# First stage of a four-stage transformer kernel: block inversion moved from VectorE to GpSimd, an instruction order per engine, and smaller stages on TensorE

## The chip, the cores and the metric

The kernel runs on one core of a Trainium2 chip. Its time is the device time of one execution in microseconds (us); shown are the median and the extremes of several runs. Engines: TensorE (PE; its weight loads are PEld in the profile), VectorE (DVE), ScalarE (ACT), GpSimd (POOL) and SyncE (SP, which here only issues DMAs). All data are float32.

## The reference, cut to what matters

The input is 16 sequences of 1024 tokens with 256 channels. Four layers follow, each with a residual and a layer norm. The first two, and the head of the third, are the stage that changes:

```python
# layer 0: causal linear attention, MLP, then a quantised 256x256 product
x = layer_norm(inputs, ln1_scale, ln1_bias)
q, k, v = (einsum('bsd,dhm->bshm', x, w) for w in (wq, wk, wv))
phi_q, phi_k = relu(q) + 1e-3, relu(k) + 1e-3
kv  = cumsum(einsum('bshm,bshd->bshmd', phi_k, v), axis=1)
num = einsum('bshm,bshmd->bshd', phi_q, kv)
den = einsum('bshm,bshm->bsh', phi_q, cumsum(phi_k, axis=1))
x = einsum('bshm,hmd->bsd', num / den[..., None], wo) + inputs
y = gelu(layer_norm(x, ...) @ w1 + b1) @ w2 + b2        # then x + y, residual, norm
xd = fp6_quantised(x); out = xd @ wd.T + bias           # residual, norm
# layer 1, head: three projections, causal convolutions of 4 taps, silu
q, k, v = (silu(causal_dwconv(hs @ W, conv_w)) for W, conv_w in ...)
q, k = l2norm(q), l2norm(k); beta = sigmoid(hs @ Wb)
# per chunk of 32 tokens and head: inverse of a unit lower triangular 32x32 block
A   = where(tri_lo_strict, (k * beta) @ k.T, 0)
inv = solve_triangular(eye + A, eye, lower=True, unit_diagonal=True)
```

The later stages use `inv` in a recurrence over chunks, add long and short convolutions, a gate and an expert layer.

## The kernel before, in words

The program has four stages one behind the other: `phase_a` (everything above), `phase_b` (convolutions of the third layer), `phase_c` (recurrence and gate) and `phase_d` (experts). Each begins when all engines have left the one before. Only `phase_a` changes.

`phase_a` handles a sequence in 4 steps of 256 tokens (two tiles of 128), 64 steps in all. One step goes through some forty named stages ("ln1", "qkv", "scores0", ..., "conv", "inverse3"). The steps are pipelined by software. A table called `shares` gives each stage its place in a step, and `pipelined` lays the stages of successive steps over each other; `PERIOD` is how far one step is behind the next in these units. The result is **one** list, `order`, and every engine runs through the same list, issuing its own part of each stage. An engine executes strictly in its list's order, and each instruction waits on semaphores for what it needs; nothing is held back for a due time.

PSUM has 8 banks of 128x512. `PsumPlan` deals them out in turn to the products, in the order in which TensorE reaches them. A product waits until the bank's previous one was read.

The parts that the change touches:

- **Inversion.** All 128 blocks of 32x32 of a sequence stand one to a partition: A and T are [128, 32, 32]. After the last step of a sequence, `gather` loads the blocks from DRAM. Then for column j = 1..30 one product (`product` = row j of A times column j of T, j x (31-j) elements) and one in-place addition to T follow, 60 dependent instructions in all. They are dealt out as `inverse0` to `inverse3` over four steps of the pipeline: 12 in the first and 16 in each of the other three. In the trace they are the lines L979 (product) and L982 (addition) on VectorE. A `Chain` makes each wait for the one before.
- **Convolution.** `conv` (L932) is 18 instructions on VectorE, scalar_tensor_tensor of 128x256, all operands in SBUF. They fill `cv`; its three parts q, k, v are ready after the 14th, 16th and 18th. TensorE's `qkvT` (L1171, transposes) waits for them part by part.
- **Attention.** `attn` is one stage and one bank: per tile t a product with the running state (L1126), then 16 with the masked scores (L1135). `scores0`, `scores1` take four banks each (L1109); VectorE masks them (L897).
- **mlp1, mlp2, qkv, qkv1, qkvT** are one stage each on TensorE. `mlp2` (L1053, a_w,a_hidden) is 16 products that take all eight rows of weights for tile 0, then for tile 1.
- **GpSimd** has the small rstd chains of the four layer norms (L636 to L639), two residual sums (L646, L647, L655) and `powers` (L665 to L680).

Of the kernel before, what the change touches and what calls it, by code (L numbers as in the profile page):

```python
# [275 lines left out]
def phase_a(nc, w, k, x, scratch, batches, banks):  # L276
# [3 lines left out]
    PERIOD = 10.437  # L280
# [14 lines left out]
    shares = [("load", 1.52), ("ln1_stats", 0.73), ("ln1", 3.18), ("xnT", 4.13), ("qkv", 1.6), ("cum", 1.28),  # L295
              ("den", 0.01), ("phikT", 1.69), ("dS", 0.43), ("rdenT", 0.89), ("scores0", 1.65), ("scores1", 2.85),
              ("attn", 0.57), ("wo", 0.57), ("ln2_stats", 1.42), ("ln2", 1.98), ("x1nT", 0.94), ("mlp1", 0.95),
              ("mlp2", 0.06), ("lnA_stats", 1.49), ("lnA", 0.97), ("quant", 2.97), ("xdT", 2.15), ("ffn", 0.47),
              ("lnB_stats", 2.29), ("lnB", 4.0), ("xbT", 1.39), ("qkv1", 0.11), ("beta", 4.14), ("conv", 1.31),
              ("qkvT", 1.43), ("squares", 2.59), ("powers", 1.48), ("kT", 0.02), ("gram", 1.54), ("keep", 2.06),  # L300
              ("gather", 33.88), ("inverse0", 2.71), ("inverse1", 2.74), ("inverse2", 2.76), ("inverse3", 0.01)]
    run = partial(run_pipelined, written=WRITTEN)
    order = pipelined(shares, STEPS, sum(share for _, share in shares) / PERIOD)
    jobs_of = {
        "xnT": ["xnT"], "qkv": ["q", "k", "v"], "den": ["den"], "phikT": ["phikT"], "dS": ["dS"], "rdenT": ["rdenT"],
        "scores0": [f"scores0{r}" for r in range(STRIPS)], "scores1": [f"scores1{r}" for r in range(STRIPS)],
        "attn": ["attn"], "wo": ["wo"],
        "x1nT": ["x1nT"], "mlp1": [f"mlp1{j}" for j in range(GELUS)], "mlp2": ["mlp2"],
        "xdT": ["xdT"], "ffn": ["ffn"], "xbT": ["xbT"], "qkv1": ["raw0", "raw1", "raw2"],
        "beta": ["beta"], "qkvT": ["qkvT0", "qkvT1", "qkvT2"], "kT": ["kT"], "gram": ["G0", "G1"],  # L310
    }
    plan = PsumPlan(order, jobs_of, banks.count, batches)
# [14 lines left out]
    with ExitStack() as ctx:  # L327
# [100 lines left out]
        with nc.Block() as block:  # L428
# [56 lines left out]
            def _(pe):  # L485
                pe.wait_ge(w_turned, 1)
                for b in range(C):
# [6 lines left out]
                 "state_ready", "masked_used",  # L494
# [55 lines left out]
        def _(sp):  # L550
# [63 lines left out]
            run(sp, order, batches, {"load": load, "lnB": store_xb, "xbT": store_xbT, "qkvT": store_qv, "kT": store_kn,  # L614
# [16 lines left out]
        def _(pool):  # L631
# [52 lines left out]

            stages = {
# [11 lines left out]
        def _(act):  # L697
# [138 lines left out]
        def _(dve):  # L836
# [129 lines left out]
            def invert(piece):  # L966

                def stage(i, s):
# [6 lines left out]
                    for j in columns_of[m]:  # L975
# [7 lines left out]
                        if j < CUT - 2:  # L983
                            link(ins)
# [1372 lines left out]
```

## Time and profile before

| | |
|---|---|
| Median of 3 runs | 5134.18 us (5132.64 to 5137.41) |
| The profiled execution's own time | 5120.81 us |
| Its span in the trace | 5119.1 us |
| Mean granted TensorE clock | 0.957 of full |
| Busy: PE, PEld | 4617.7 us (90%), 3868.0 us (76%) |
| Busy: DVE, ACT, POOL | 4119.6 us (80%), 2802.1 us (55%), 2775.1 us (54%) |
| `phase_a` in the trace | about 36 to 3053 us |

A matmul in these rows is pipelined with the next, so PE's busy time overlaps itself at the edges. Float32 products appear as two or more records each. "Idle before" is the time that the engine stood still ahead of a group, and the name behind the arrow is what ended it.

### The profile page before, as it was taken

Reading aid. Unit: us, or ns where it says so; the run is one execution under the profiler, and the core shown is the slowest. Engines: PE = TensorE matmul, PEld = TensorE weight load, DVE = VectorE, ACT = ScalarE, POOL = GpSimd, SP = SyncE. Lnnn points to the kernel's source line nnn. Section 1 sums busy time; section 2 is a strip of 40 time slices with the busy share of each in tenths; the row PEclk is TensorE's granted clock in tenths of the full one; section 3 lists DMA queues with packets and bytes.
Section 4 is the critical chain, followed back from the end, with each engine's and each line's share of the span. In section 5 each row is a group of like instructions: output and inputs, shape, how many; then the busy total and the mean of one; then the engine's idle time right before and its main releaser. Section 6 shows DMA issues by size and latency. Waiting matters only on the chain. (4 is left out here: it accounts for less than half of the span.)

```text
span 5119.1 us, 116501 instructions
## 1 busy us (share of the span) xinstructions
PE 4617.7 (90%) x42012; PEld 3868.0 (76%) x42012; DVE 4119.6 (80%) x12689; ACT 2802.1 (55%) x6469; POOL 2775.1 (54%) x3719
## 2 busy tenths in 40 slices
PE   5999999999999999999999939969999999999969
PEld 4887877877887787788788738947777777777745
DVE  4789889988888988888898852239999999999961
ACT  2554555555555555555555522137777777777751
POOL 1344444443444444444344423229999999999980
PEclk9999999999999999999999969979999999999979
DMA  1121222222122122112212237743444444444410
GB/s 44 42 62 51 62 59 59 58 65 60 47 63 66 51 62 63 55 58 64 59 48 65 60 78 164 181 123 113 121 116 116 121 114 118 120 114 120 118 60 27
DMA packets 738175, 416.03 MB, mean 81 GB/s; under 512 B 341764, under 2 KB 725576, under 8 KB 737608
## 3 DMA queue, kind: packets, MB, share of 16 engines
q1 hardware_dynamic: 667144, 372.92, 25.7%
q10 hardware_dynamic: 65664, 16.78, 1.4%
q0 software_dynamic: 4800, 18.88, 1.2%
q8 instruction: 343, 5.62, 0.5%
q14 instruction: 224, 1.84, 0.1%
HBM read 220.98 MB, written 187.43 MB: 80 GB/s over the span
## 5 line engine op out<-in xcount | busy, mean ns | idle before, releaser
L636 POOL TENSOR_TENSOR a_shift<-a_mean_var,a_eps 128x2 f32<-128x2 f32 x256 | 71.7, 280 | 1418.1 <-DVE a_mean_var L918 1418.1
L932 DVE SCALAR_TENSOR_TENSOR a_cv<-a_raw,a_taps,a_cv 128x256 f32<-128x256 f32 x1152 | 566.9, 564 | 10.1 <-DVE a_scaled L864 9.9
L1151 PE MATMUL a_bank<-a_turned,a_w 128*128 128x256 f32 x2048 | 455.9, 381 | 4.8 <-ACT a_turned L719 4.8
L1053 PE MATMUL a_bank<-a_w,a_hidden 128*128 128x256 f32 x2048 | 452.8, 379 | 0.9 <-ACT a_hidden L764 0.9
L1151 PEld LDWEIGHTS a_bank<-a_turned,a_w 128*128 128x128 f32 x2048 | 383.9, 190 | 59.1 <-ACT a_turned L719 8.8
L1053 PEld LDWEIGHTS a_bank<-a_w,a_hidden 128*128 128x128 f32 x2048 | 384.1, 190 | 51.3 <-ACT a_hidden L764 1.7
L1738 POOL TENSOR_TENSOR c_stats<-c_l2sq,half 128x16 f32<-128x16 f32 x128 | 374.7, 2927 | 73.0 <-DVE c_l2sq L1912 73.0
L1745 POOL TENSOR_TENSOR c_expd<-c_e,c_logit 128x16 f32<-128x16 f32 x128 | 371.6, 2903 | 0.0
L897 DVE TENSOR_TENSOR a_masked<-a_bank,keep_causal 128x512 f32<-128x512 f32 x512 | 317.5, 682 | 61.2 <-PE a_bank L1109 59.7
L2063 PE MATMUL c_bank<-c_u,c_grams 128*32 128x64 f32 (+2 forms) x3072 | 232.3, 219 | 57.4 <-ACT c_u L1784 57.3
L780 ACT ACTIVATE a_raw<-a_bank 128x512 f32<-128x512 f32 x192 | 114.9, 598 | 300.4 <-PE a_bank L1044 300.4
L667 POOL TENSOR_TENSOR a_coef<-a_base,a_powers_half 128x24 f32<-128x24 f32 x64 | 274.9, 4295 | 5.0
L1896 DVE BATCH_NORM_STATS2 c_bn<-c_src 128x6 f32<-128x64 f32 x2048 | 272.0, 211 | 3.9
L2063 PEld LDWEIGHTS c_bank<-c_u,c_grams 128*32 128x32 f32 (+2 forms) x3072 | 182.4, 107 | 111.9 <-issue 83.1
L792 ACT ACT_TABLE_LOAD x62 | 79.5, 1283 | 334.5 <-PE a_bank L1171 334.5
L982 DVE TENSOR_TENSOR a_T<-a_T,a_product 128x30 f32<-128x30 f32 (+14 forms) x480 | 242.3, 505 | 16.5
L1787 ACT ACTIVATE c_z<-c_bank 32x256 f32<-32x256 f32 x512 | 192.1, 375 | 106.3 <-PE c_bank L2017 58.6
L1430 PE MATMUL b_bank<-b_window,b_matrix 128*128 128x128 f32 x1024 | 226.0, 397 | 10.0 <-POOL b_window L1322 10.0
L1430 PEld LDWEIGHTS b_bank<-b_window,b_matrix 128*128 128x128 f32 x1024 | 211.6, 212 | 23.4 <-issue 10.6
L637 POOL TENSOR_TENSOR a_rstd<-a_shift,neg_half 128x2 f32<-128x2 f32 x256 | 205.3, 802 | 20.0
L1784 ACT ACTIVATE c_u<-c_bank 32x256 f32<-32x256 f32 x512 | 192.1, 375 | 43.1 <-PE c_bank L2024 33.9
L764 ACT ACTIVATE a_hidden<-a_bank,a_b 128x256 f32<-128x256 f32 x512 | 200.3, 480 | 19.1 <-PE a_bank L1151 18.2
(291 smaller groups left out, 13094.0 us busy)
## 6 DMA issues: line engine op xcount, KB each, us to landing
a_x<-in_x SPq DMA_DIRECT2D x64, 256.0 KB, 3.0
scratch_xb<-a_xb SPq DMA_DIRECT2D x64, 256.0 KB, 2.1
scratch_xbT<-a_turned SPq DMA_DIRECT2D x128, 128.0 KB, 2.2
scratch_qT<-a_cv SPq DMA_DIRECT2D x128, 128.0 KB, 2.2
scratch_v<-a_qkv_rows SPq DMA_DIRECT2D x64, 256.0 KB, 2.2
scratch_kn<-a_kn SPq DMA_DIRECT2D x64, 256.0 KB, 2.1
scratch_vb<-a_qkv_rows SPq DMA_DIRECT2D x64, 256.0 KB, 2.1
scratch_kT<-a_kT SPq DMA_DIRECT2D x128, 128.0 KB, 2.6
```

What stands on the lines that cost most here:

```text
L637: link(pool.tensor_tensor(rstd[s][:, which], shift[s][:, which], k["neg_half"][:, 0:T], ALU.pow))
L667: link(pool.tensor_tensor(coef[s][:], base[s][:], powers_half[:], ALU.pow))
L897: ins = dve.tensor_tensor(masked[t][:, r], src[:].rearrange("p (h i) -> p h i", h=C * 2), k["keep_causal"][:, None, :].broadcast_to([P, C ...
L932: ins = dve.scalar_tensor_tensor(cv[s][:, n, c], raw[s][:, n, c, j:j + TOK], taps[:, n, c, j:j + 1], cv[s][:, n, c], ALU.mult, ALU.add)
L982: ins = dve.tensor_tensor(rest, rest, part, ALU.add)
L1053: ins = pe.matmul(dst[:, t * D:(t + 1) * D], src[s][:, c, tile_cols(t)], weight[:, c], start=(c == 0), stop=(c == chunks - 1))
L1151: ins = pe.matmul(dst[:, at:at + TOK], w1_sb[:, c, m * P:(m + 1) * P], x1nT[s][:, c], start=(c == 0), stop=(c == C - 1))
L1430: ins = pe.matmul(dst[:, (c - q * QUAD) * N:(c - q * QUAD + 1) * N], taps_of, window[h][:, :, c], start=True, stop=True)
L1738: pool.tensor_tensor(stats[s % SLOTS][:, :, 0, :, 3], l2sq[s % SLOTS][:].rearrange("p (s h) -> p h s", s=SRC), k["half"][:].rearrange("p ( ...
L1745: pool.tensor_tensor(expd[sl][:], e_base[:].rearrange("p (h e) -> p h e", h=H), logit[sl][:], ALU.pow).then_inc(N["exp_ready"], 1)
L1896: ins = dve.bn_stats(bn[sl][:, n * H + h], src[sl][:, n, h * DH:(h + 1) * DH])
L2063: ins = pe.matmul(psum[CHAIN[m]][rows, h * DH:(h + 1) * DH], grams[sl][known, h % 2, h // 2, 0, rows], u_sb[sl][known, h], start=False, st ...
```

## The change

**The inversion's instructions are the same, but GpSimd issues them.** `invert` moves from the VectorE block to the GpSimd block, with its waits and its chain (after: L712 product, L715 addition). In GpSimd's order the four pieces of a step stand together, right behind the rstd chain of layer norm B.

**Each engine has an order of its own.** `shares` is replaced by `starts`, a table with one dictionary per engine of times in us, and `PERIOD` is 43.40. `interleaved` sorts each engine's stages by them. PSUM banks are dealt in TensorE's order. The times only set the order.

**Products are separate entries on TensorE**: q, k, v; mlp10 to mlp13; mlp2 by tile (mlp20, mlp21); raw0 to raw2; qkvT0 to qkvT2. Others can so stand between them.

**Each attention half has a bank.** `attn0` and `attn1` are filled, waited for and evacuated on their own; the masks of tile 0 wait for `attn0` and not for a semaphore of their own (`masked_used` goes). ScalarE copies the two halves with two activations of 128x256 and not one of 128x512.

```diff
-    PERIOD = 10.437
+    PERIOD = 43.40
...
-    shares = [("load", 1.52), ("ln1_stats", 0.73), ("ln1", 3.18), ("xnT", 4.13), ("qkv", 1.6), ("cum", 1.28),
...
+    starts = {
...
+        "dve": {"ln1_stats": 4.06, "q": 22.61, "k": 23.44, "cum": 24.34, "den": 27.77, "dS": 31.04, "rdenT": 32.22,
...
-    order = pipelined(shares, STEPS, sum(share for _, share in shares) / PERIOD)
+    order = {eng: interleaved(own, STEPS, PERIOD) for eng, own in starts.items()}
...
-    plan = PsumPlan(order, jobs_of, banks.count, batches)
+    plan = PsumPlan(order["pe"], jobs_of, banks.count, batches)
...
+            def invert(piece):
+
+                def stage(i, s):
+                    m = s * PIECES + piece
+                    A_, T_ = A_sets[i % 2], T_sets[i % 2]
+                    if m == 0:
+                        pool.wait_ge(sets_in[i % 2], 32 * (i // 2 + 1))
+                        link(pool.memset(T_[:].rearrange("p a b -> p (a b)")[:, 0::CUT + 1], 1.0))
+                        return
+                    for j in columns_of[m]:
+                        below_j = slice(j + 1, CUT)
+                        shape = [P, j, CUT - 1 - j]
+                        part = product[:, 0:shape[1] * shape[2]].rearrange("p (c r) -> p c r", c=j)
+                        link(pool.tensor_tensor(part, A_[:, j:j + 1, below_j].broadcast_to(shape),
+                                               T_[:, 0:j, j:j + 1].broadcast_to(shape), ALU.mult))
+                        rest = T_[:, 0:j, below_j]
+                        ins = pool.tensor_tensor(rest, rest, part, ALU.add)
+                        if j < CUT - 2:
+                            link(ins)
+                    if m == STEPS * PIECES - 1:
+                        ins.then_inc(S["inverse_ready"], 1)
+                return stage
...
+            def attention(i, s):
+                for t in range(T):
+                    src = full(act, i, s, f"attn{t}")[:].rearrange("p (c n) -> p c n", c=C)
+                    freed(act.activation(attnT[s][:, :, tile_cols(t)], src[:, :, tile_cols(t)], ACT.Copy), s, f"attn{t}")
...
                 def stage(i, s):
                     if not_first(i, s, 1):
-                        if t == 0:
-                            dve.wait_ge(S["masked_used"], seq(i, s) - 1)
-                        else:
-                            computed(dve, *back(i, s, 1), "attn")
+                        computed(dve, *back(i, s, 1), f"attn{t}")
...
-            def attention(i, s):
-                dst = open_bank(i, s, "attn", "v", *(f"scores0{r}" for r in range(STRIPS)))
-                for t in range(T):
+            def attention(t):
+                def stage(i, s):
+                    dst = open_bank(i, s, f"attn{t}", "v", *(f"scores{t}{r}" for r in range(STRIPS)))
...
-            def mlp2(i, s):
-                token_major(i, s, "mlp2", w2_sb, hidden, f"mlp1{GELUS - 1}", M)
+            def mlp2(t):
+                def stage(i, s):
+                    dst = open_bank(i, s, "mlp2", f"mlp1{GELUS - 1}") if t == 0 else psum[plan.bank(s, "mlp2")]
```

GpSimd, before, in the middle of a step: the rstd chain of a layer norm (four rows), two residual sums, the next chain.

```order
L636 TENSOR_TENSOR a_shift<-a_mean_var,a_eps 128x2
L637 TENSOR_TENSOR a_rstd<-a_shift,neg_half 128x2
L638 TENSOR_TENSOR a_shift<-a_mean_var,a_rstd 128x2
L639 TENSOR_TENSOR a_shift<-a_shift,a_minus_one 128x2
L646 TENSOR_TENSOR a_x<-a_x 128x512
L647 TENSOR_TENSOR a_x<-a_x,a_b 128x512
```

GpSimd, after, in a step that holds columns 7 to 14: the rstd chain of layer norm B, then the inversion without a break.

```order
L650 TENSOR_TENSOR a_shift<-a_mean_var,a_eps 128x2
L651 TENSOR_TENSOR a_rstd<-a_shift,neg_half 128x2
L652 TENSOR_TENSOR a_shift<-a_mean_var,a_rstd 128x2
L653 TENSOR_TENSOR a_shift<-a_shift,a_minus_one 128x2
L712 TENSOR_TENSOR a_product<-a_A,a_T 128x168
L715 TENSOR_TENSOR a_T<-a_T,a_product 128x7x24
L712 TENSOR_TENSOR a_product<-a_A,a_T 128x184
L715 TENSOR_TENSOR a_T<-a_T,a_product 128x8x23
L712 TENSOR_TENSOR a_product<-a_A,a_T 128x198
L715 TENSOR_TENSOR a_T<-a_T,a_product 128x9x22
```

Ten further rows of L712 and L715 follow there before the next chain.

VectorE, before, around the convolution (L932): pieces of the inversion stand behind it and between the masks.

```order
L864 TENSOR_TENSOR a_scaled<-a_bank,a_phiq 128x512
L932 SCALAR_TENSOR_TENSOR a_cv<-a_raw,a_taps,a_cv 128x256 x18
L979 TENSOR_TENSOR a_product<-a_A,a_T 128x210
L982 TENSOR_TENSOR a_T<-a_T,a_product 128x21x10
L979 TENSOR_TENSOR a_product<-a_A,a_T 128x198
L982 TENSOR_TENSOR a_T<-a_T,a_product 128x22x9
L897 TENSOR_TENSOR a_masked<-a_bank,keep_causal 128x512 x4
```

VectorE, after: masks of scores1, `below`, the sum behind the quantised product (L950), the statistics of layer norm B, and then the convolution (L975).

```order
L940 TENSOR_TENSOR a_masked<-a_bank,keep_causal 128x512 x4
L1001 TENSOR_TENSOR a_below<-a_bank,a_drop_block 128x4x32 x2
L950 TENSOR_TENSOR a_xs<-a_bank,a_resid 128x512
L958 BN_STATS a_stats<-a_xs 128x6 x2
L961 BN_AGGR a_mean_var<-a_stats 128x2 x2
L975 SCALAR_TENSOR_TENSOR a_cv<-a_raw,a_taps,a_cv 128x256 x18
L950 TENSOR_TENSOR a_xs<-a_bank,a_x 128x512
```

The statistics that start GpSimd's chain B now stand directly ahead of the convolution.

TensorE, before, from mlp2 to the next step's q.

```order
L1053 MATMUL a_bank<-a_w,a_hidden 128x256 x16
L1171 MATMUL a_bank<-ident,a_cv 128x128 x12
L1109 MATMUL a_bank<-a_phiq_own,a_phik 128x256 x8
L1034 MATMUL a_bank<-ident,a_xb 128x128 x4
L1126 MATMUL a_bank<-a_scaled,a_state 128x128 x2
L1135 MATMUL a_bank<-a_masked,a_v_own 32x128 x16
L1126 MATMUL a_bank<-a_scaled,a_state 128x128 x2
L1135 MATMUL a_bank<-a_masked,a_v_own 32x128 x16
L1044 MATMUL a_bank<-a_turned,a_wq 128x256 x4
```

TensorE, after, from the quantised product (ffnT) to the next step's q.

```order
L1069 MATMUL a_bank<-a_ffnT,a_turned 128x256 x4
L1145 MATMUL a_bank<-a_scaled,a_state 128x128 x2
L1151 MATMUL a_bank<-a_masked,a_v_own 32x128 x16
L1176 MATMUL a_bank<-a_w,a_hidden 128x256 x8
L1050 MATMUL a_bank<-ident,a_xb 128x128 x4
L1176 MATMUL a_bank<-a_w,a_hidden 128x256 x8
L1196 MATMUL a_bank<-ident,a_cv 128x128 x4
L1050 MATMUL a_bank<-ident,a_xn 128x128 x4
L1196 MATMUL a_bank<-ident,a_cv 128x128 x8
L1060 MATMUL a_bank<-a_turned,a_wq 128x256 x4
```

The transposes of `cv` (L1196) now stand directly ahead of the next q, and `kT` and the Gram products, which stood back to back, have scores1 and attn0 between them.

## Rows read from the trace of the kernel before

**Rows 1.** Busy time by stretch: stretch, length, PE PEld DVE ACT POOL, PEclk, DMA, GB/s.

```profile
104.39:314.32 209.93, 200.81 (x1616) 172.03 (x1612) 158.90 (x395) 107.84 (x214) 78.45 (x117) 0.98 0.14 41
401.24:2870.55 2469.31, 2312.28 (x19340) 1980.61 (x19337) 2188.85 (x5377) 1300.96 (x2539) 1061.35 (x1405) 0.97 0.20 59
2870.55:3052.60 182.05, 103.03 (x868) 86.08 (x864) 132.30 (x354) 60.04 (x120) 65.17 (x69) 0.78 0.22 65
```

**Rows 2.** Busy time by stretch: two steps that follow each other.

```profile
2003.50:2045.70 42.20, 41.02 (x364) 35.41 (x356) 38.38 (x98) 23.78 (x47) 18.80 (x26) 1.00 0.19 54
2045.70:2093.20 47.50, 44.48 (x368) 38.23 (x360) 42.31 (x102) 24.30 (x48) 20.02 (x27) 0.93 0.17 49
```

**Rows 3.** Who waited for whom, TensorE, 401.24:2870.55: us in total, times, longest us.

```profile
PE a_bank L1069 <- DVE a_scaled L854: 54.3, 28, 2.0
...
PE a_bank L1200 <- ACT a_kT L817: 41.5, 54, 0.8
```

**Rows 4.** Timeline of TensorE in these two steps: start us, length us, group, idle before.

```profile
2020.49 1.89 PE L1053 MATMUL a_bank<-a_ffnT,a_turned 128*128 128x256 f32 x8
...
2063.41 1.85 PE L1069 MATMUL a_bank<-a_head_of,a_scaled 128*128 128x8 f32 x8 [2.03 <-DVE a_scaled L854]
...
2066.00 3.49 PE L1053 MATMUL a_bank<-a_ffnT,a_turned 128*128 128x256 f32 x8
```

**Rows 5.** Timeline of VectorE at the end of the stage.

```profile
2999.13 7.21 DVE L932 SCALAR_TENSOR_TENSOR a_cv<-a_raw,a_taps,a_cv 128x256 f32<-128x256 f32 x18
...
3030.68 0.19 DVE L979 TENSOR_TENSOR a_product<-a_A,a_T 128x30 f32<-128x30 f32 x1
...
3052.37 0.21 DVE L982 TENSOR_TENSOR a_T<-a_T,a_product 128x30 f32<-128x30 f32 x1
```

**Rows 6.** GpSimd's groups by shape, 200:3000: busy us, mean ns, idle before.

```profile
L637 POOL TENSOR_TENSOR a_rstd<-a_shift,neg_half 128x2 f32<-128x2 f32 x242 | 193.9, 801 | 18.9
...
L646 POOL TENSOR_TENSOR a_x<-a_x 128x512 f32<-128x512 f32 x61 | 81.3, 1333 | 0.0
...
L675 POOL TENSOR_TENSOR a_kn<-a_qkv_rows,a_coef 128x512 f32<-128x512 f32 x62 | 64.7, 1044 | 4.9
...
L666 POOL TENSOR_TENSOR a_base<-a_base,a_one_base 128x8 f32<-128x8 f32 x62 | 12.7, 205 | 4.8
```

**Rows 7.** Timeline of VectorE: sum and statistics, convolution, one addition of the inversion.

```profile
2022.42 0.69 DVE L907 TENSOR_TENSOR a_xs<-a_bank,a_resid 128x512 f32<-128x512 f32 x1 [0.35 <-PE a_bank L1053]
...
2023.93 0.25 DVE L918 BATCH_NORM_AGGREGATE a_mean_var<-a_stats 128x2 f32<-128x6 f32 x2
...
2026.11 8.93 DVE L932 SCALAR_TENSOR_TENSOR a_cv<-a_raw,a_taps,a_cv 128x256 f32<-128x256 f32 x18 [0.16 <-DVE a_scaled L864]
...
2044.91 1.30 DVE L982 TENSOR_TENSOR a_T<-a_T,a_product 128x168 f32<-128x168 f32 x1
```

**Rows 8.** Timeline of GpSimd at the same places.

```profile
2025.74 1.28 POOL L646 TENSOR_TENSOR a_x<-a_x 128x512 f32<-128x512 f32 x1
2027.09 1.33 POOL L647 TENSOR_TENSOR a_x<-a_x,a_b 128x512 f32<-128x512 f32 x1
...
2044.65 1.36 POOL L655 TENSOR_TENSOR a_resid<-a_xa,a_ffn_bias 128x512 f32<-128x512 f32 x1 [1.57 <-ACT a_xa L707]
```

**Rows 9.** Timeline of TensorE: mlp2, transposes of cv, xb, the second attention half.

```profile
2032.61 7.07 PE L1053 MATMUL a_bank<-a_w,a_hidden 128*128 128x256 f32 x32
2039.51 1.47 PE L1171 MATMUL a_bank<-ident,a_cv 128*128 128x128 f32 x12
...
2041.99 0.66 PE L1034 MATMUL a_bank<-ident,a_xb 128*128 128x128 f32 x4
2042.77 1.08 PE L1135 MATMUL a_bank<-a_masked,a_v_own 128*32 128x128 f32 x32
2043.78 0.71 PE L1126 MATMUL a_bank<-a_scaled,a_state 128*128 128x128 f32 x4
...
2045.79 1.99 PE L1044 MATMUL a_bank<-a_turned,a_wq 128*128 128x256 f32 x8
```

More of the change, by code:

```diff
@@ L312, in phase_a @@
-    plan = PsumPlan(order, jobs_of, banks.count, batches)
+        "attn0": ["attn0"], "attn1": ["attn1"], "wo": ["wo"],
+        "x1nT": ["x1nT"], "mlp20": ["mlp2"],
+        "xdT": ["xdT"], "ffn": ["ffn"], "xbT": ["xbT"],
+        "beta": ["beta"], "kT": ["kT"], "gram": ["G0", "G1"],
+    }
+    jobs_of |= {job: [job] for job in [f"mlp1{j}" for j in range(GELUS)] + [f"{n}{j}" for n in ("raw", "qkvT") for j in range(3)]}
+    plan = PsumPlan(order["pe"], jobs_of, banks.count, batches)
     HEADS, HEAD = 4, D // 4
@@ L1137, in attention, with mlp1, stage @@
                                                 start=(fresh and c == 0 and o == 0), stop=(o == 1), skip_group_check=True)
[L1138 to L1140 removed]
+                    fill(ins, s, f"attn{t}")
+                return stage
             def wo(i, s):
[L1143 to L1146 removed]
+                in_sbuf(pe, i, s, "attn0")
+                token_major(i, s, "wo", wt["wo"], attnT, "attn1")
+            def mlp1(j):
+                def stage(i, s):
                     dst = open_bank(i, s, f"mlp1{j}", "x1nT")
@@ L1206, in _ @@
                 "beta": beta, "kT": turn_keys, "gram": gram,
-                "xnT": turn("xnT", xn, S["xn_ready"]), "qkv": qkv, "den": head_sums, "phikT": phik_turn,
+                "xnT": turn("xnT", xn, S["xn_ready"]), "q": qkv("q"), "k": qkv("k"), "v": qkv("v"), "den": head_sums, "phikT": phik_turn,
                 "dS": d_states, "rdenT": turn_rden, "scores0": scores(0), "scores1": scores(1),
-                "attn": attention, "wo": wo,
-                "x1nT": turn("x1nT", x1n, S["x1n_ready"]), "mlp1": mlp1, "mlp2": mlp2,
+                "attn0": attention(0), "attn1": attention(1), "wo": wo,
+                "x1nT": turn("x1nT", x1n, S["x1n_ready"]), "mlp20": mlp2(0), "mlp21": mlp2(1),
                 "xdT": turn("xdT", xd, S["xd_ready"]), "ffn": ffn,
-                "xbT": turn("xbT", xb, S["xb_ready"]), "qkv1": qkv1, "qkvT": qkv_turn,
+                "xbT": turn("xbT", xb, S["xb_ready"]),
             }
-            run(pe, order, batches, stages)
+            stages |= {f"mlp1{j}": mlp1(j) for j in range(GELUS)}
+            stages |= {f"raw{n}": qkv1(n, name) for n, name in enumerate(("Wq", "Wk", "Wv"))}
+            stages |= {f"qkvT{n}": qkv_turn(n) for n in range(3)}
+            run(pe, order["pe"], batches, stages)
     banks.count = plan.after(batches)
```

118 lines of the change are left out of this document (52 added, 66 removed), and 5 rows, old and new, of the table starts.

## Prediction, made before the kernel ran

> **What bounds the kernel now.** I read the page first, then the busy times by stretch, the waits of TensorE, and timelines of single steps.
>
> The change touches only the first stage. In it 54 steps run with an inversion in flight, from 401.24 to 2870.55 us: 2469.31 / 54 = 45.73 us a step [rows 1]. Five steps before the first inversion took 209.93 / 5 = 41.99 us. TensorE is busy for 42.8 us of 45.73, VectorE for 40.5, ScalarE for 24.1, GpSimd for 19.7 (the busy times of [rows 1] by 54). So TensorE bounds a step and VectorE nearly does. The reader is to see both in two neighbours [rows 2]: 42.2 us at full clock with VectorE at 38.4 of it, then 47.5 us at a mean granted clock of 0.93 with VectorE at 42.3 busy.
>
> What lies between them is in the waits [rows 3, 4]: TensorE waits for VectorE's `scaled` ahead of L1069 28 times, 54.3 us in total and up to 2.0, and behind such a wait it runs at its lower level, 1.2 GHz: the same group takes 3.49 us and not 1.89. A mean of 0.93 in 47.5 us is 6.7 us at half speed, which costs 3.3 us. A third wait, 0.77 us for `kT`, is in each of the 54 steps [rows 3]: a step without it would take 42.0 - 0.8 = 41.2 us.
>
> The end of the stage, 2870.55 to 3052.6, is a drain of 182 us, and at its end VectorE runs the last inversion alone, 3030.68 to 3052.58 = 21.9 us [rows 1, 5].
>
> **The change part by part.**
>
> *The inversion leaves VectorE.* That frees 21.9 us a sequence, 5.5 a step, or more where GpSimd was in the way. VectorE falls to about 35 of 42 us and is not the bound. The in-trace evidence for what this buys are the 42.0 us of the steps without inversion [rows 1].
>
> *It arrives on GpSimd.* The trace has no such instruction there, so its cost comes from its neighbours [rows 6]: 205 ns for 8 elements, 1333 ns for a sum of two full operands of 512 elements (1.28 us at its quicker in [rows 8]), 1044 ns for a product with a repeated operand. I take 197 ns plus 1.66 ns an element for the product and 2.1 ns for the addition, and 0.07 us between dependent ones (1.28 behind 2025.74, next at 2027.09 [rows 8]), 0.08 for rounding. A sequence has 4960 elements in 30 columns: 4960 x 3.76 ns + 60 x 0.275 = 35.1 us, in four steps 5.4, 10.7, 11.2 and 7.8. The bounds: as fast as on VectorE, 21.9; or, if short rows and the strided column of T make elements dearer, 44.4: an operand read in full and not repeated costs a factor 1333 / 1044 = 1.28 [rows 6], two such steps would be 1.6, and I price half as much again, + 9.3. GpSimd is busy for 19.7 + 8.8 = 28.5 of some 44 us, so it is not the bound; what it holds up is the question.
>
> *What it holds up.* [Rows 7, 8]: an addition of the inversion on VectorE, where one of these instructions takes 21.9 / 60 = 0.37 us on the average with its gap, took 1.30 us and ended at 2046.21, just behind GpSimd's L655 (2044.65 to 2046.01). The convolution, 18 instructions, took 8.93 us where L646 and L647 ran beside its first 2.3 us, and 7.21 us with GpSimd idle [rows 5]. So a VectorE instruction with two operands in SBUF stands still while GpSimd streams, and one gets through between two of GpSimd's: end to end of L646 and L647 is 1.40 us, against 1.27 + 0.08 alone, and a convolution instruction alone is 7.21 / 18 = 0.40. I take one convolution instruction for each GpSimd instruction of d us, every d + 0.14 us.
>
> The Trainium skill says the same in "SBUF — State Buffer", section "Who interferes with whom": a VectorE instruction with two SBUF inputs and a GpSimd instruction that reads SBUF exclude each other, and the later one fully blocks. The trace agrees (1.30 us for some 0.37); by this rule the convolution is what pays, and without it the forecast would be the first rival's.
>
> By the order after, the convolution stands right behind the statistics of layer norm B, and GpSimd's inversion right behind that norm's rstd chain, 0.80 + 3 x 0.2 + gaps = 1.6 us later [rows 6]. So four convolution instructions (1.6 us) run free and the other 14 meet the inversion. First 14 inversion instructions of the four steps: 12 with 560 elements, then 1442, 1610 and 882 elements in pairs: 14 x 0.337 + 1442 x 3.76 ns = 10.1 us, 10.8, 8.0, and in the first step 12 x 0.337 + 2.1 = 6.1 and then free. Convolution: 8.5, 11.7, 12.4, 9.6 us and not 7.2.
>
> *Who waits for that.* TensorE's qkvT needs `cv`, and in its order q, k, v, wo and all else of the next step queue behind it. Both paths start where TensorE ends ffnT. VectorE: sum and statistics 1.7 us (2022.42 to 2024.10, [rows 7]), then the convolution, 0.1 latency: 9.0 us if free. TensorE [rows 9]: an attention half 1.7 us (0.71 and 1.01), mlp2 6.9, xb 0.8, two thirds of qkvT 0.9, xn 0.5: 10.8 us. The slack is 1.8 us. The convolution's 8.5, 11.7, 12.4, 9.6 turn it into stalls of 0, 2.7, 3.4 and 0.6: 6.7 us a sequence, at a new place, L1196. Bounds: none at all, or 14.8 with the dearer elements.
>
> *TensorE's own order.* kT's 0.8 us of waiting goes, since scores1 and attn0 stand between kT and the Gram products: 41.2 us a step. The separate entries add no matmul. I add 0.8 us for more changes of tile shape (attn0, Gram, ffnT, attn1 alternate) and small waits for banks; bounds 0 and 2. So 42.0 us a step.
>
> *Clock.* Stalls of 2.7 and 3.4 us in three bits with transposes between are near the 2.8 us (0.77 + 2.03) that precede the lower level in [rows 4]. I take 3.4 us at half speed once a sequence, 1.7 us; bounds 0 and 10.
>
> *Banks, ScalarE, SyncE.* A bank per half is one product more in 38; mlp1's banks are read while scores0 runs. ScalarE gains one activation a step, some 0.3 us beside 24 of 42. SyncE issues the same DMAs; its loads are queued ahead of their use by most of a step, and its wait for the inversion comes once a sequence behind the piece that it waits for. Nothing for the three.
>
> *The drain.* The last inversion is alone on its engine: 35.1 - 21.9 = +13 us. The one before it, also on GpSimd now, shares the drain with `powers`: +4. Bounds 0 and 30.
>
> *Sum.* 4 x 42.0 + 6.7 + 1.7 = 176.4 us a sequence, 44.1 a step. (45.73 - 44.1) x 54 = 88 us less, 17 more in the drain: 71 us. The profiled execution took 5120.8 us; the median of the runs is 13 above it. The same difference off the median gives 5134.2 - 71 = 5063 us.
>
> **The rivals.**
>
> *The lock does not bite (faster).* GpSimd's inversion is quicker than I think, or slips beside the convolution. No stall: 42.0 us a step, 3.73 x 54 - 17 = 184 us, 4950 us. For it: the five steps at 41.99. Against it: the 1.30 us in [rows 7].
>
> *The stalls cost the clock each time (slower).* If three steps of a sequence fall to 1.2 GHz for 6.8 us as in [rows 2], that is 10.2 and not 1.7 us: 184.9 us a sequence, 46.2 a step, +27 and +17 in the drain: 5178 us. For it: 0.93 in the 47.5 us step. Against: the bits are shorter than 2.03.
>
> *GpSimd is dear on short rows (slower).* Half as much again per element: convolutions of 9.6, 14.5, 15.4, 11.3 us, stalls 0.6, 5.5, 6.4, 2.3 = 14.8, clock 10.2: 193.0 us, 48.25 a step, +136, drain +26: 5296 us. It decides from where stalls and clock together pass 13.6 us a sequence: 4 x 45.73 - 168 = 14.9, less 17 us of drain over 13.5 sequences. For it: T's column is read with a stride of 32 elements and rows get as short as one element, and no row shows either on GpSimd. Against: 8 rows of 64 elements cost no more than long ones [rows 6].
>
> The Trainium skill's "GPSIMD Engine Reference", "Performance pitfalls for Q7 kernels", states half as much again for reads with a step of over 8 bytes. No run here shows it yet; it would make this rival true for the products alone. The same page's "Performance versus the Vector engine" has GpSimd 1.96 times slower on additions, which as an estimate would make 43 us of 21.9.
>
> **How the numbers follow.** What a measurement of this kernel can tell from no change is about 0.2%, 10 us. The forecast has 0.40 (5020 to 5110), the first rival 0.28, the clock 0.14, dear rows 0.18. The range reaches from the first rival to just beyond the clock's case, 4945 to 5190, which leaves most of dear rows and a little below out, 0.2. Faster: 0.28 and nearly all of the forecast, 0.67. Within 0.2%: the stretch between the forecast and the clock's case, 0.08. Slower: 0.25.
>
> **What the changed profile would show.** Right: L712 and L715 at 0.2 to 0.7 us and 35 us a sequence; the convolution at 8.5 to 12.4 us in a cycle of four steps; TensorE waiting ahead of L1196 for a_cv in two or three of four steps, and no longer ahead of L1069 and L1226; steps of about 42, 45, 47 and 43 us; the drain 17 us longer. Wrong: no wait ahead of L1196 (first rival), a clock under 0.97 with equal stalls (second), L712 or L715 over 0.8 us (third), or TensorE waiting elsewhere, for ScalarE or for GpSimd's rstd behind an inversion.

## The result, and the profile after

| | before | after |
|---|---|---|
| Median of the runs | 5133.41 us (5127.47 to 5137.41, 4 runs) | 5007.69 us (4997.87 to 5012.58, 4 runs) |
| Profiled execution: own time, span | 5120.81, 5119.1 | 5012.58, 5010.9 |
| A step with an inversion in flight | 45.73 | 43.37 |
| Drain, to the end of the last inversion | 182.0 | 194.2 |

The ratio is 0.9754, 95% interval 0.9736 to 0.9771. The medians differ by 126 us and the profiled executions by 108: the one of before was 13 us quicker than its median, the one of after 5 slower.

The busy times by stretch of after, the steady stretch first, then the drain, then five steps in a row; columns as in [rows 1]:

```profile
404.93:2746.71 2341.78, 2249.72 (x19339) 1919.53 (x19338) 1965.46 (x4552) 1311.58 (x2593) 1471.31 (x2230) 1.00 0.21 62
2746.71:2940.00 193.29, 102.76 (x867) 85.43 (x865) 95.10 (x222) 65.16 (x128) 127.70 (x197) 0.74 0.21 63
1442.53:1487.37 44.84, 41.88 (x363) 35.69 (x362) 38.52 (x86) 24.34 (x49) 29.82 (x42) 1.00 0.18 52
1487.37:1530.08 42.71, 41.88 (x363) 35.68 (x362) 36.47 (x86) 23.28 (x49) 27.46 (x43) 1.00 0.19 54
1530.08:1571.76 41.68, 41.13 (x360) 35.38 (x358) 34.90 (x88) 24.16 (x49) 22.72 (x37) 1.00 0.30 93
1571.76:1615.13 43.37, 41.23 (x355) 35.14 (x356) 35.66 (x80) 25.43 (x49) 28.64 (x45) 1.00 0.19 53
1615.13:1660.02 44.89, 41.93 (x362) 35.68 (x361) 38.47 (x86) 24.33 (x49) 29.72 (x42) 1.00 0.18 51
```

In these five rows TensorE is busy for 41 to 42 us, whatever the length of the step: what varies is its waiting. The steps repeat in a cycle of four, 41.7, 43.4, 44.9 and 42.7 us. The granted clock is 1.00 where it was 0.97. TensorE's waits in 404.93:2746.71 (us in total, times, longest us), against [rows 3]:

```profile
PE a_bank L1196 <- DVE a_cv L975: 69.7, 109, 1.4
PE a_bank L1128 <- DVE a_masked L940: 13.6, 53, 0.6
PE a_bank L1060 <- ACT a_turned L760: 3.9, 13, 0.3
```

Before had three large waits and not two. [Rows 3] and the prediction leave out one ahead of the first product of a step, once a sequence:

```profile
PE a_bank L1044 <- DVE a_phiq L841: 43.4, 13, 3.4
```

All three, 54.3, 43.4 and 41.5 us, are gone. The new one is ahead of L1196, for the convolution. Its length in the cycle follows from VectorE's timeline, one row a step (light, then two heavy ones), the first against 7.21 and 8.93 us in [rows 5, 7]:

```profile
1562.27 7.18 DVE L975 SCALAR_TENSOR_TENSOR a_cv<-a_raw,a_taps,a_cv 128x256 f32<-128x256 f32 x18
1603.75 10.88 DVE L975 SCALAR_TENSOR_TENSOR a_cv<-a_raw,a_taps,a_cv 128x256 f32<-128x256 f32 x18
1647.83 11.69 DVE L975 SCALAR_TENSOR_TENSOR a_cv<-a_raw,a_taps,a_cv 128x256 f32<-128x256 f32 x18
```

TensorE at the end of the second of them. It stands still three times, 0.57 + 0.44 + 0.87 = 1.9 us:

```profile
1611.77 0.63 PE L1196 MATMUL a_bank<-ident,a_cv 128*128 128x128 f32 x4 [0.57 <-DVE a_cv L975]
1612.23 0.60 PE L1050 MATMUL a_bank<-ident,a_xn 128*128 128x128 f32 x4
1613.28 0.63 PE L1196 MATMUL a_bank<-ident,a_cv 128*128 128x128 f32 x4 [0.44 <-DVE a_cv L975]
1614.78 0.63 PE L1196 MATMUL a_bank<-ident,a_cv 128*128 128x128 f32 x4 [0.87 <-DVE a_cv L975]
1615.24 1.89 PE L1060 MATMUL a_bank<-a_turned,a_wq 128*128 128x256 f32 x8
```

The last row, 1.89 us, is at full clock, where the wait of 2.03 us was followed by 3.49 [rows 4]. The trace of before has 35 stretches at half clock in its 54 steps, 153.6 us in all: 13 at the 13 waits for `phiq`, 22 at the 28 waits for `scaled`. The trace of after has 4, 13.7 us in all. Three of the 4 begin in the heaviest step of a cycle, behind its waits of 1.35 and 0.50 us; eleven other cycles have the same waits without a fall.

This says where the gain of the steady stretch lies (2469.31 - 2341.78 = 127.5 us). As an estimate, a stretch at half clock costs half its length: 77 us before, 7 after, so some 70 of the 127.5 us are the clock. The other part is waiting itself, 155 us before and 92 after over all lines. The two together are 5 us more than the gain.

GpSimd's timeline beside the second convolution, where the inversion starts behind the four short instructions, and two rows from the drain:

```profile
1605.52 0.32 POOL L653 TENSOR_TENSOR a_shift<-a_shift,a_minus_one 128x2 f32<-128x2 f32 x1
1605.80 0.72 POOL L712 TENSOR_TENSOR a_product<-a_A,a_T 128x168 f32<-128x168 f32 x1
1606.60 0.60 POOL L715 TENSOR_TENSOR a_T<-a_T,a_product 128x168 f32<-128x168 f32 x1
1607.28 0.57 POOL L712 TENSOR_TENSOR a_product<-a_A,a_T 128x184 f32<-128x184 f32 x1
...
2906.50 0.24 POOL L712 TENSOR_TENSOR a_product<-a_A,a_T 128x30 f32<-128x30 f32 x1
...
2940.64 0.26 POOL L715 TENSOR_TENSOR a_T<-a_T,a_product 128x30 f32<-128x30 f32 x1
```

Five convolution instructions had ended when the inversion began; the other 13 ended beside it, and 13 of the inversion's began by then. The last two rows are the first product and the last addition of the stage's last inversion, which runs alone: 34.4 us.

### The profile page after: what moved, and what is told of

The parts are those of the page before. It is cut to its first block and busy times, and to the rows that moved or that the text cites. A ratio compares the mean times of both kernels' runs of the same rounds, so it can differ in the third digit from the quotient of the medians.

```text
span 5010.9 us, 116744 instructions
## 1 busy us (share of the span) xinstructions
PE 4560.6 (91%) x42012; PEld 3809.5 (76%) x42012; DVE 3858.2 (77%) x11713; ACT 2815.8 (56%) x6533; POOL 3246.9 (65%) x4695
## 5 line engine op out<-in xcount | busy, mean ns | idle before, releaser
L650 POOL TENSOR_TENSOR a_shift<-a_mean_var,a_eps 128x2 f32<-128x2 f32 x256 | 59.2, 231 | 980.1 <-DVE a_mean_var L961 976.7
L975 DVE SCALAR_TENSOR_TENSOR a_cv<-a_raw,a_taps,a_cv 128x256 f32<-128x256 f32 x1152 | 617.3, 611 | 0.1
L1176 PE MATMUL a_bank<-a_w,a_hidden 128*128 128x256 f32 x2048 | 469.5, 383 | 0.0
L1176 PEld LDWEIGHTS a_bank<-a_w,a_hidden 128*128 128x128 f32 x2048 | 379.5, 190 | 58.5 <-issue 12.5
L712 POOL TENSOR_TENSOR a_product<-a_A,a_T 128x30 f32<-128x30 f32 (+14 forms) x480 | 285.7, 595 | 34.1
L760 ACT ACTIVATE a_turned<-a_bank,a_ln_bias,a_ln_scale 128x256 f32<-128x256 f32 x256 | 130.5, 560 | 313.6 <-PE a_bank L1050 313.6
L715 POOL TENSOR_TENSOR a_T<-a_T,a_product 128x30 f32<-128x30 f32 (+14 forms) x480 | 263.6, 549 | 37.6
L1459 PEld LDWEIGHTS b_bank<-b_window,b_matrix 128*128 128x128 f32 x1024 | 211.8, 212 | 25.1 <-issue 12.4
L1784 POOL TENSOR_TENSOR c_mixed<-c_src,c_coef 128x256 f32<-128x256 f32 x256 | 175.6, 707 | 46.1 <-DVEq L1962 46.1
L651 POOL TENSOR_TENSOR a_rstd<-a_shift,neg_half 128x2 f32<-128x2 f32 x256 | 186.3, 728 | 20.1
```

What stands on the lines that cost most here:

```text
L712: link(pool.tensor_tensor(part, A_[:, j:j + 1, below_j].broadcast_to(shape), T_[:, 0:j, j:j + 1].broadcast_to(shape), ALU.mult))
L715: ins = pool.tensor_tensor(rest, rest, part, ALU.add)
L975: ins = dve.scalar_tensor_tensor(cv[s][:, n, c], raw[s][:, n, c, j:j + TOK], taps[:, n, c, j:j + 1], cv[s][:, n, c], ALU.mult, ALU.add)
L1176: ins = pe.matmul(dst[:, t * D:(t + 1) * D], hidden[s][:, m, tile_cols(t)], w2_sb[:, m], start=(m == 0), stop=(m == M - 1))
L1459: ins = pe.matmul(dst[:, (c - q * QUAD) * N:(c - q * QUAD + 1) * N], taps_of, window[h][:, :, c], start=True, stop=True)
```

## The experiments

Each ran beside the kernel before on its chip. Three batches: before's medians in them were 5139.46, 5130.43 and 5131.47 us. "Mean step" is of the 54 steady steps in the run's own trace, "half" the stretches at half clock in them. The runs with memsets and with no inversion have two executions each (those with memsets 32 us apart), the others four to eight. "After, again" was expected at 5000 to 5015 us. "All but the move" is after with the inversion on VectorE: the new orders, the split products and the two attention banks stay.

| run | median us | ratio to before, 95% | mean step | half |
|---|---|---|---|---|
| the move alone | 5116.01 | 0.9960 (0.9949 to 0.9971) | 45.24 | 34 |
| all but the move, first places | 5334.78 | 1.0392 (1.0371 to 1.0414) | 49.44 | 57 |
| all but the move, placed | 5106.16 | 0.9954 (0.9940 to 0.9967) | 45.51 | 29 |
| after, products whole | 5117.55 | 0.9968 (0.9957 to 0.9980) | 45.06 | 19 |
| after, one bank | 5025.81 | 0.9793 (0.9778 to 0.9808) | 43.50 | 2 |
| after, again | 5002.66 | 0.9751 (0.9738 to 0.9764) | 43.35 | 2 |
| inversion as memsets | 4984.29 | 0.9706 (0.9663 to 0.9749) | 42.42 | 5 |
| no inversion | 4954.06 | 0.9647 (0.9623 to 0.9671) | 42.99 | 12 |
| half beside the convolution | 4964.98 | 0.9671 (0.9655 to 0.9687) | 42.65 | 1 |
| off it, products whole, one bank | 4994.13 | 0.9730 (0.9715 to 0.9744) | 43.00 | 2 |
| off the convolution | 4914.68 | 0.9584 (0.9571 to 0.9597) | 41.92 | 0 |
| off it, last inversion on VectorE | 4902.34 | 0.9556 (0.9543 to 0.9569) | 41.90 | 0 |

### Which part does it?

**The move alone**: before, with `invert` in the GpSimd block, in the same common list.

```diff
         @block.gpsimd
+            def invert(piece):
...
         @block.vector
-            def invert(piece):
```

> The kernel before, with the inversion issued by GpSimd at the same places of the one common list; no order per engine, no separate entries, one bank for attention. Theory (relief: VectorE without the inversion lets TensorE set the step): steps of 42.2 to 43.5 us in the steady part and not 45.7, 4990 to 5060 us with 15 us more drain. Rival (the orders and the separate entries brought the gain): steps stay near 45.7, 5130 to 5160 us.

It gives 0.4%, and 5116.01 us lies outside both ranges: 56 us above the theory's, 14 below the rival's. VectorE is relieved (2007 us busy in the steady stretch against 2189 [rows 1]), and yet the step shrinks by 0.5 us only. TensorE's waits, 404.21:2847.18:

```profile
PE a_bank L1044 <- DVE a_phiq L868: 41.5, 13, 3.2
PE a_bank L1200 <- ACT a_kT L844: 41.5, 54, 0.8
PE a_bank L1069 <- DVE a_scaled L881: 11.8, 28, 0.4
```

The wait for `scaled` falls from 54.3 to 11.8 us. Those for `phiq` and `kT` stand as they did before (43.4 and 41.5 us), and the stretches at half clock are 34 and not 35. The order puts these two waits there, not VectorE's load: relief leaves them, and the runs with the new orders do not have them.

**All but the move**, inversion on VectorE, its four pieces behind layer norm A's statistics, ahead of the last sum of states, ahead of the quantising, and behind the masks.

```diff
         "dve": {"ln1_stats": 4.06,
...
+                "inverse0": 368.70, "inverse1": 378.10, "inverse2": 381.50, "inverse3": 393.30},
         "pool": {"ln1_stats": 7.57,
...
-                 "inverse0": 363.60, "inverse1": 366.07, "inverse2": 368.02, "inverse3": 369.99},
```

> The changed kernel, with the inversion back on VectorE, its pieces behind the statistics of norm A, behind the squares, ahead of the quantisation and behind the masks of scores0. Relief theory: VectorE is full again (35 + 6 to 7 of some 42 us), steps of 43.5 to 45.5 us, 5030 to 5110 us. Rival (orders and entries): steps of 42 to 43 us, under 5000 us.

A miss: slower than before by 3.9%. TensorE waited for `x_d`, up to 5.3 us, in each step (194.5 us in 54 waits); two pieces stood ahead of the quantising, in the fullest stretch of VectorE. The places of the pieces were my choice and not part of the change, so a second run has them where VectorE had been seen idle.

```diff
-               "keep": 225.13, "gather": 229.25, "inverse3": 371.41},
+               "keep": 225.13, "gather": 229.25, "inverse3": 414.81},
...
-                "inverse0": 368.70, "inverse1": 378.10, "inverse2": 381.50, "inverse3": 393.30},
+                "inverse0": 367.70, "inverse1": 371.10, "inverse2": 387.20, "inverse3": 398.10},
```

> The orders of the changed kernel with the inversion back on VectorE, as in the run with the orders alone, but its four pieces of a step stand where VectorE has been seen idle (behind the third layer norm's statistics, k, the quantising and the block of kept products), and SyncE's store of the inverse a step later, so that its queue does not stand. Theory 1 (the first try was slow by its places: pieces ahead of the quantising, 5.3 us of wait at x_d, and half clock behind it): most of that goes, steps of 44 to 46 us, 5030 to 5150 us. Theory 2 (VectorE, at 39.4 us of work in a step of 43, has no room wherever the pieces stand, so the orders are worth something only with the move): still 5200 us or more.

The first theory holds. All but the move gives 0.5%: the convolution is at 7.18 us in every step, but VectorE's other results are late now. Another placing of the pieces may do better; two were tried.

```profile
PE a_bank L1128 <- DVE a_masked L913: 83.6, 54, 2.2
PE a_bank L1088 <- DVE a_scaled L873: 42.2, 54, 1.1
```

**Products whole**: after, with the split products of a stage in one place of TensorE's order again.

```diff
-               "mlp21": 100.79, "xdT": 130.65, "ffn": 136.27, "xbT": 143.37, "raw0": 158.28, "raw1": 161.48,
-               "raw2": 163.92, "beta": 174.66, "qkvT0": 190.80, "qkvT1": 192.06, "qkvT2": 192.69,
+               "mlp21": 96.60, "xdT": 130.65, "ffn": 136.27, "xbT": 143.37, "raw0": 158.28, "raw1": 158.29,
+               "raw2": 158.30, "beta": 174.66, "qkvT0": 192.04, "qkvT1": 192.06, "qkvT2": 192.69,
```

> The changed kernel with the products of one stage in one place of TensorE's order again (both halves of mlp2, the three of qkv1, the three turned products). Theory 1 (the split gives TensorE work while the late convolution and the turns are awaited): the wait ahead of L1196 grows by the length of what stood there, 0.9 us for mlp2's half and 0.5 for the turned third, and VectorE's and ScalarE's results are awaited ahead of the raw products: 43.9 to 45.5 us a step, 5030 to 5120 us. Theory 2 (the split does nothing, the move and the other places do it all): 5000 to 5015 us.

The time is at the first theory's far end, 5117.55 us: of the change's 2.5%, 0.3% is left. TensorE's waits, 406.88:2840.08, and two steps of it:

```profile
PE a_bank L1196 <- DVE a_cv L975: 77.5, 109, 1.1
PE a_bank L1167 <- ACT a_turned L760: 60.0, 54, 1.1
```

```profile
1583.18:1625.63 42.45, 41.09 (x360) 35.54 (x358) 33.17 (x88) 22.91 (x49) 24.36 (x36) 1.00 0.28 88
1670.38:1718.33 47.95, 43.71 (x363) 37.09 (x362) 37.27 (x86) 24.30 (x49) 31.97 (x42) 0.96 0.17 48
```

The loss is not where the theory had it: the wait for the convolution grows by 8 us only. A second appears ahead of mlp1, 1.1 us in each step, for ScalarE's evacuation of the turned x1n. In after the third raw product (1.89 us) stands between x1n's transposes and mlp1; here all three stand earlier. And the half clock is back in the heavy steps: 19 stretches and not 4. That products must be split for this is not shown. Before has them whole, with other products between the two, and only 3.0 us of this wait in all; raw products kept whole but placed directly ahead of mlp1 were not tried.

**One bank** for both attention halves in after, one evacuation for both, and the masks' semaphore of before (of the edit, the line that says it):

```diff
-        "attn0": ["attn0"], "attn1": ["attn1"],
+        "attn0": ["attn"],
```

> The changed kernel with both halves of attention in one bank again and one evacuation for both on ScalarE. Theory 1 (a bank for each half only lets ScalarE start on the first half early, and wo is not awaited for anything now): within 0.2% of the changed kernel, 4995 to 5015 us. Theory 2 (without it the bank is held from the first half to the end of the second, 10 us and more with other products between, and wo waits for the later evacuation): 0.3 to 1 us of wait a step ahead of wo, 5020 to 5060 us.

The time is in the second theory's range, but its wait ahead of wo is not in the trace. 23 us slower than after again: mean step 43.50 against 43.35, which is 8 us of it, 7 in what follows the steps and 4 ahead of them. The bank is a small part of the gain.

### Is the stall the convolution's, and is that GpSimd's doing?

**Memsets in place of the inversion's instructions**, of about the same length (593 elements take 0.59 us); the inverse is left out and T is zero.

```diff
-                        link(pool.tensor_tensor(part, A_[:, j:j + 1, below_j].broadcast_to(shape),
-                                               T_[:, 0:j, j:j + 1].broadcast_to(shape), ALU.mult))
...
-                        ins = pool.tensor_tensor(rest, rest, part, ALU.add)
+                        n = j * (CUT - 1 - j)
+                        link(pool.memset(A_[:].rearrange("p a b -> p (a b)")[:, 0:125 + 2 * n], 0.0))
+                        ins = pool.memset(A_[:].rearrange("p a b -> p (a b)")[:, 0:125 + 5 * n // 2], 0.0)
```

> The changed kernel, with the inversion's products and additions replaced by as many memsets of about the same length, which read nothing (the inverse is left out; T is zero). Lock theory (GpSimd's reads hold up the convolution): convolution 7.2 us in every step, no wait ahead of L1196, steps of 41.7 us, 1.7 x 54 = 90 us less than the changed kernel, about 4920 us. Rival (the small rstd chains of GpSimd queue behind the inversion, or GpSimd is simply late): steps stay at 43.4 us, about 5008 us.

**No inversion**: these two instructions and their waits left out, T zero.

```diff
-                    for j in columns_of[m]:
...
```

> The changed kernel without the inversion's 60 instructions (T is zero, gather and store stay). Steps of 41.7 us as in the lock theory's case, and 35 us less drain than the changed kernel: about 4885 us. If TensorE had other waits hidden behind the convolution's, the steps stay above 42.2 us and the time above 4910.

On the mechanism both agree with the lock: the convolution takes 7.18 us in every step, beside the memsets too, and the wait ahead of L1196 is gone. So GpSimd's being busy is not what costs: instructions that only write SBUF leave the convolution alone, those of the inversion, which read and write it, do not. VectorE and GpSimd in the memset run:

```profile
1428.90 7.18 DVE L971 SCALAR_TENSOR_TENSOR a_cv<-a_raw,a_taps,a_cv 128x256 f32<-128x256 f32 x18
1430.93 0.48 POOL L710 MEMSET a_A<- 128x461 f32 x1
1431.47 0.55 POOL L711 MEMSET a_A<- 128x545 f32 x1
```

The Trainium skill, "SBUF — State Buffer", section "Who interferes with whom", has VectorE's two-input instruction contend only with a GpSimd instruction that reads SBUF, not with one that writes only. By that rule, the trace agrees (7.18 us).

On the size both missed, by 64 and 69 us. Their steps are 41.5 to 42.1 us for the most part, but in 5 and 12 of the 54 the clock falls. Why is below, under what was not expected.

**Off the convolution**: after, with two pieces of each step behind `powers`, where VectorE masks scores out of PSUM, and two behind the convolution, with a wait for its end.

```diff
-               "keep": 225.13, "gather": 229.25, "inverse3": 371.41},
+               "keep": 225.13, "gather": 229.25, "inverse3": 414.81},
...
-                 "inverse0": 363.60, "inverse1": 366.07, "inverse2": 368.02, "inverse3": 369.99},
+                 "inverse0": 393.90, "inverse1": 394.00, "inverse2": 401.60, "inverse3": 401.70},
...
                     m = s * PIECES + piece
+                    if piece == 2:
+                        pool.wait_ge(S["cv_ready"], 3 * min(seq(i, s) + 5, batches * STEPS))
```

> The changed kernel with GpSimd's inversion put where the convolution does not run: two pieces of each step behind the powers, beside the masking of the scores, and two behind the convolution, with a wait for its end. Theory 1 (an operation of the inversion that reads and writes SBUF holds up VectorE's convolution, whose lateness is the stall of 0 to 2.7 us ahead of the turned products): the convolution takes 7.2 us in every step, the wait at L1196 goes, steps of 41.7 to 42.5 us as without the inversion, 167.6 to 169.5 us for four in place of 172.6, less 42 to 68 us in all: 4940 to 4970 us. Theory 2 (it is GpSimd's own load of 1470 us in 2342 that sets the step, so the pieces make another of its results late wherever they stand: the variance roots of the first layer norm behind the powers, or of the third behind the convolution): the stall reappears ahead of the products that wait for those, 5010 us or more.

The first theory, and more than it gave: 4914.68 us, 88 less than after beside it. Its steady stretch, one cycle, and all of TensorE's waits over 2 us in total:

```profile
403.33:2666.93 2263.60, 2231.57 (x19336) 1919.95 (x19336) 1824.66 (x4551) 1310.69 (x2593) 1407.73 (x2228) 1.00 0.22 64
1492.93:1534.61 41.68, 41.13 (x357) 35.34 (x357) 33.80 (x83) 24.31 (x49) 26.69 (x45) 1.00 0.27 80
1534.61:1576.09 41.48, 40.93 (x357) 35.27 (x357) 33.16 (x84) 24.30 (x49) 21.77 (x39) 1.00 0.22 68
1576.09:1618.21 42.12, 41.57 (x361) 35.79 (x361) 34.05 (x85) 24.30 (x49) 26.40 (x41) 1.00 0.19 55
```

```profile
PE a_bank L1061 <- ACT a_turned L761: 16.1, 54, 0.3
PE a_bank L1129 <- DVE a_masked L941: 13.9, 54, 0.6
```

The masks take 0.68 us beside the inversion's pieces, as without them. GpSimd issues the same instructions, TensorE is busy for 98.6% of the stretch, and the clock never falls.

**Half beside the convolution**: the same without the wait.

> The kernel off the convolution without GpSimd's wait for the convolution's end: two of the four pieces of a step (some 4 to 5.6 us of GpSimd) run beside the convolution again. Lock theory: each operation of these pieces lets one of VectorE's through, so the convolution takes 8 to 10 us and not 7.2, which is within the slack or 1 us beyond it: steps of 41.7 to 43 us, 4915 to 4945 us. Rival (the wait itself did harm or good by when GpSimd comes to its next stage): outside of that.

The time is 20 us beyond the lock theory's range, so by its range the rival's. The trace speaks for the lock in kind: the convolution takes 8.37, 10.07, 9.94 and 7.71 us and the steps 41.5, 43.5, 43.4 and 41.7. With after's four this gives the slack. In after the excess over the run off the convolution is 0, 1.9, 2.7 and 0.6 us for convolutions of 7.18, 10.88, 11.69 and 9.57: each is the convolution less 8.98 us, so 1.8 us of lateness are free. Here it is 1.4 and 1.3 for 10.07 and 9.94, 0.3 more than that, for a reason that is not shown.

**Off it, with products whole and one bank**: both undone in the run off the convolution.

> The kernel off the convolution with the products whole and attention in one bank: only the move of the inversion and the orders are left of the change, at the better place. Theory 1 (with the stall ahead of L1196 gone, split products have nothing left to cover): 4910 to 4935 us. Theory 2 (they cover the evacuations of ScalarE as well): 1 us or more a step, 4970 us or more.

The second theory: 79 us more than off the convolution. The wait for ScalarE ahead of mlp1 is back, 60.0 us in 54 times, without any for the convolution. So that wait comes from the places of TensorE's products and not from the late convolution. The place of the inversion is worth 88 us with the products split (5002.66 to 4914.68) and 123 or more with them whole (5117.55 to 4994.13, where the second has one bank as well).

**Last inversion on VectorE**: as off the convolution, but `invert` of the last sequence is issued by VectorE.

```diff
         @block.gpsimd
...
+                    if i == batches - 1:
+                        return
...
         @block.vector
...
+            def invert(piece):
...
+                    if i < batches - 1:
+                        return
```

> As the kernel off the convolution, and the inversion of the last sequence alone goes to VectorE, which is idle in the drain. Theory 1 (the drain ends with this inversion, of 34.4 us on GpSimd and 21.9 us on VectorE before): 12.5 us less than the kernel off the convolution, 4928 to 4957 us. Theory 2 (something else ends the drain as well, or the two take the same time where nothing runs beside them): within 3 us of it.

12.3 us less, as the first theory has it (12.5): the drain ends with this inversion. The time itself lies 26 us below the range, which was set from the forecast for the run off the convolution. It is the best version, 2.0% below the changed kernel.

## Why the prediction was right, point by point

The direction and the mechanism held: TensorE stands ahead of L1196 for a convolution that GpSimd's inversion holds up, in three of four steps. The size did not: 126 us of gain and not 71. The 5007.69 us lie 12 below the forecast's own 5020 to 5110, between it and the first rival, and inside the full range because that reached down to the rival's 4945. By point:

- **What bounds the step** (TensorE at 42.0 once nothing is late): right. With nothing late it is 41.9 us (off the convolution).
- **The price on GpSimd**, 35.1 us a sequence: right, 34.4 alone. Where nothing runs beside them, 168 elements took 0.48 to 0.50 us for the product and 0.51 to 0.53 for the sum, where the two lines through 8 and 512 elements gave 0.48 and 0.55. So the first rival's quicker GpSimd and the third's dear rows were both wrong; the column read with a stride cost nothing that shows at this size.
- **The convolution**, 8.5, 11.7, 12.4 and 9.6 us: 7.18, 10.88, 11.69 and 9.57. In the three heavy steps the alternation of one for one is in the trace. Two sizes were off: five instructions ran free and not four, and the cadence is d + 0.08 us, not d + 0.14. In the light step it failed: the inversion waits 2.73 us for its DMA, and its first product, which starts beside the convolution, does not get a turn until the convolution has ended (see the last section).
- **The slack**, 1.8 us: right to a tenth.
- **The stalls**, 6.7 us a sequence: 5.2 (0, 1.9, 2.7, 0.6), by these convolutions.
- **The clock**, 1.7 us a sequence: 4 stretches of 3.4 us in 13.5 sequences cost some 0.5. This term was too large, and the second rival failed with it. With whole products it would have had a point: 19 stretches, in steps with waits of 1.09 + 0.93 + 0.85 and of 0.31 + 0.88 + 0.87 us.
- **The waits of before**: read incompletely. `phiq`, 43.4 us and 13 of the 35 stretches at half clock, is missing, and "behind such a wait it runs at its lower level" held for 22 of 28. The sum did not suffer, since it starts from the 42.0 us of steps without an inversion.
- **The drain**, +17: 12.2 to the end of the inversion, which is the last one's 12.5; the 4 for the one before it did not come. 15.6 to the end of the program.
- **The sum**: 173.5 us a sequence and not 176.4, which is 39 us more gain in 54 steps than the 88. With + 15.6 in the drain and 3.7 at the start the profiled executions differ by 108, where I had 71. The medians' 126 hold 18 more, from where the two profiled executions stand among the runs.

The term most mis-sized is the stalls (1.5 us of the 2.9 a sequence), then the clock. What the prediction did not see is which part earns the gain. It set most of it down to VectorE's relief, yet the move alone gives 23 us, all but the move 24, both with whole products 14, and only all of it 126. Each leaves waits that another part removes. The move alone leaves `phiq` and `kT`, which the orders remove. All but the move leaves `masked` and `scaled`, which relief removes but for 13.6 us of `masked`. Whole products, where they were placed, leave ScalarE's evacuation.

## What to carry to other kernels

Where an engine is within a few per cent of the bound, relief for it, its order and the neighbours' pieces can be worth much only together, as here: list all waits, the rare long ones too, and look for the next before pricing one. An operation moved to GpSimd should stand beside VectorE instructions that read PSUM, or behind the ones with two inputs in SBUF with a wait: 88 us for one wait and five numbers here. And between a product and the one that waits for its evacuation, put a product of another stage: without it that wait was 1.1 us a step here.

## What was not expected of the hardware

**A small GpSimd instruction can wait for a whole train of VectorE's.** Without any inversion the kernel was 39 us slower than with one off the convolution (32 by the ratios to before). In 12 of its 54 steps an addition of 8 elements, elsewhere 0.23 to 0.48 us, took 4.64 us. VectorE and GpSimd in such a step, and TensorE behind it:

```profile
546.61 0.49 DVE L205 TENSOR_SCALAR a_quant_p<-a_quant_y 128x256 int32<-128x256 int32 x2
547.01 0.49 DVE L209 TENSOR_SCALAR a_quant_p<-a_quant_p 128x256 f32<-128x256 f32 x2
547.42 0.76 DVE L214 SCALAR_TENSOR_TENSOR a_quant_r<-a_quant_p,a_quant_y 128x256 f32<-128x256 f32 x2
547.63 4.64 POOL L680 TENSOR_TENSOR a_base<-a_base,a_one_base 128x8 f32<-128x8 f32 x1
...
551.44 0.76 DVE L233 TENSOR_TENSOR a_xd<-a_quant_r,a_quant_scale 128x256 f32<-128x256 f32 x2
552.34 4.17 POOL L681 TENSOR_TENSOR a_coef<-a_base,a_powers_half 128x24 f32<-128x24 f32 x1
```

```profile
554.56 0.95 PE L1193 MATMUL a_bank<-a_Wb,a_turned 128*128 128x4 f32 x8
558.22 1.09 PE L1202 MATMUL a_bank<-ident,a_kn 128*128 128x128 f32 x4 [2.71 <-POOL a_kn L689]
```

And in the next step, where it came ahead of the train:

```profile
593.82 0.24 POOL L680 TENSOR_TENSOR a_base<-a_base,a_one_base 128x8 f32<-128x8 f32 x1
594.13 0.52 DVE L209 TENSOR_SCALAR a_quant_p<-a_quant_p 128x256 f32<-128x256 f32 x2
```

The record of 4.64 us ends 0.06 us behind the last of VectorE's 14 instructions with two inputs in SBUF. Over the steady steps of after, of the memsets and of no inversion, its length goes with its start against the nearest start of L214: at -0.19 us it took 0.33 us, at 0.00 it took 0.48, and at -0.13 or -0.12 it took 4.63 or 4.64, all 19 times. TensorE then stands 2.6 to 3.1 us for the normalised k, and behind 18 of the 19 waits it runs at 1.2 GHz: steps of some 46.4 us and not 41.7. Against the run off the convolution this makes the steady stretch 58 us longer without inversion, of the 69 lacking there, and 27 us with memsets, of 64; the rest of those 64 is not explained. After has this once, at 2627.77, and its step takes 47.15 us: the fourth of its stretches at half clock. Off the convolution it does not occur.

After has a like case in each of 15 sequences, in the light step. The inversion's first product, 30 elements and 0.24 us where it is alone, starts beside the convolution, which ends at 1569.45 in this one:

```profile
1567.32 2.23 POOL L712 TENSOR_TENSOR a_product<-a_A,a_T 128x30 f32<-128x30 f32 x1
```

It took 0.73 to 2.80 us and ended 0.10 us behind the convolution all 15 times, wherever it started against VectorE's instructions (-0.19 to +0.15 us from the nearest start). So the start alone does not decide it. In the heavy steps the same pair alternates one for one, and what decides between the two is not shown. That the trains are the cause is read from these traces; no run shifted a GpSimd instruction on purpose.
